# One order over a whole transformer block on one core, with TensorE's part in both arms of each block's branch

## The reference

```python
# 1: attention on Q, K, V reshaped to (B*H, S, D) = (64, 1024, 8); its output is projected, added and normed again
scores = jnp.einsum('bqd,bkd->bqk', Q, K) / jnp.sqrt(jnp.float32(D))
attn = jax.nn.softmax(scores, axis=-1)
ctx = jnp.einsum('bqk,bkd->bqd', attn, V)
# 2: a gated feed-forward with ternary weights, width 512
h = jax.nn.silu(_tlin(x, w1_w, w1_s)) * _tlin(x, w2_w, w2_s)
h = jax.nn.gelu(_tlin(h, h1_w, h1_s), approximate=False)
h = jax.nn.gelu(_tlin(h, h2_w, h2_s), approximate=False)
return _tlin(h, w3_w, w3_s)
# 3: gated linear attention, a scan over the time of each sequence
h = h * jnp.exp(gt)[..., None] + kt[..., None] * vt[..., None, :]
ot = jnp.einsum('bhk,bhkv->bhv', qt, h)
# 4: a mixture of 8 experts ("zones"); per sequence of 1024 rows the router takes the top 3
z = jax.nn.gelu(x @ Wa[e]) @ Wb[e]
zone_outputs = zone_outputs + z * w[:, e, None, None]
```

## Time and profile before

| | us |
|---|---|
| median of 3 runs | 1131.49 |
| lowest and highest of them | 1122.34, 1132.95 |
| the profiled execution | 1121.4 |
| its span, from the first to the last instruction | 1119.5 |
| PE busy | 1019.4 (91%) |
| ACT busy | 810.6 (72%) |
| DVE busy | 646.0 (58%) |
| POOL busy | 375.2 (34%) |

### The profile page before, as it was taken

The page is one execution under the profiler, slowest core; times in us unless marked ns, Lnnn a source line. Parts: engine busy times, 40 slices in busy tenths (PEclk is TensorE's granted clock), DMA queues, the critical chain, the costliest instruction groups (busy, mean ns, idle before and its releaser), DMA issues.

```text
span 1119.5 us, 16637 instructions
## 1 busy us (share of the span) xinstructions
PE 1019.4 (91%) x5970; PEld 509.1 (45%) x5970; DVE 646.0 (58%) x1173; ACT 810.6 (72%) x1097; POOL 375.2 (34%) x317
## 2 busy tenths in 40 slices
PE   2799999999999999999698988888788899999998
PEld 1232333333333333333276655565355536666667
DVE  3121454526344443313464999999999899995200
ACT  2699999999999999999557667565656675455441
POOL 1000010101000010100153787798679767655100
PEclk7799999999999999999899999999799999999999
DMA  5766453625455452710101101100000122011200
GB/s 126 121 113 118 92 117 63 125 60 110 77 104 96 86 106 52 121 36 15 34 1 38 38 1 39 38 1 29 28 20 1 57 57 85 1 48 29 57 29 20
DMA packets 98780, 66.90 MB, mean 60 GB/s; under 512 B 61636, under 2 KB 84964, under 8 KB 96612
## 3 DMA queue, kind: packets, MB, share of 16 engines
q1 hardware_dynamic: 98656, 65.33, 28.0%
q10 hardware_dynamic: 24, 0.25, 0.1%
HBM read 46.41 MB, written 18.87 MB: 58 GB/s over the span
## 4 chain that ended last, share of the span: by engine, by line
PE 63%; DVE 19%; POOL 5%; issue 5%; ACT 3%; SPq 1%; DMA 1%; ACTq 0%; DVEq 0%; POOLq 0%
PE PS L1481 26%; PE PS L1466 15%; DVE R L1293 8%; PE PS L1652 6%; PE PS L1515 4%; DVE R L1284 4%; POOL R L869 3%; PE PS L1641 3%; PE PS L1555 2%; PE PS L1410 2%; DVE RB L1246 1%; DVE R L1252 1%; PE PS L1579 1%; PE PS L1396 1%; DVE R L1256 1%
## 5 line engine op out<-in xcount | busy, mean ns | idle before, releaser
L922 ACT ACTIVATE R<-PS 128x1024 f32<-128x1024 f32 x512 | 474.4, 1085 | 58.4 <-PE PS L1466 57.6
L1481 PE MATMUL PS<-R 128*32 128x512 f32 x2048 | 314.1, 607 | 1.2 <-issue 1.2
L869 POOL TENSOR_TENSOR R<-R 128x512 f32<-128x512 f32 x128 | 216.1, 1705 | 50.0 <-DVE R L1293 27.1
L1293 DVE TENSOR_TENSOR_SCAN R<-R 128x512 f32<-128x512 f32 x128 | 208.6, 1630 | 0.0
L1466 PE MATMUL PS<-RA 34*128 34x512 f32 x1024 | 189.2, 447 | 20.1 <-DMA RA<-QD 19.5
L1515 PE MATMUL PS<-RB,WR 128*128 128x512 f32 x640 | 174.8, 417 | 18.4 <-DVE R L1252 12.1
L1466 PEld LDWEIGHTS PS<-RA 34*128 34x128 f32 x1024 | 77.1, 186 | 216.2 <-issue 193.5
L1515 PEld LDWEIGHTS PS<-RB,WR 128*128 128x128 f32 x640 | 122.9, 195 | 63.0 <-DVE R L1252 14.3
L1481 PEld LDWEIGHTS PS<-R 128*32 128x32 f32 x2048 | 68.0, 108 | 106.1 <-issue 94.1
L855 POOL TENSOR_TENSOR RB<-R,RB 128x512 fp32r<-128x512 f32 x48 | 75.6, 1576 | 76.6 <-ACT RB L932 68.1
L845 POOL PARTITION_ALL_REDUCE R<-R x8 | 3.0, 376 | 287.6 <-DVE R L1133 287.6
(11 more groups left out here) (129 smaller groups left out, 1005.1 us busy)
## 6 DMA issues: line engine op xcount, KB each, us to landing
RA<-QD SPq DMA_DIRECT2D x256, 64.0 KB
QD<-RA SPq DMA_DIRECT2D x128, 64.0 KB, 2.1
RA<-QD SPq DMA_DIRECT2D x64, 128.0 KB
OD<-R SPq DMA_DIRECT2D x128, 32.0 KB, 2.0
R<-OD SPq DMA_DIRECT2D x128, 32.0 KB
VD<-RC SPq DMA_DIRECT2D x16, 256.0 KB, 2.3
RC<-VD SPq DMA_DIRECT2D x16, 256.0 KB
WP<-in_Wa SPq DMA_DIRECT2D x12, 256.0 KB, 3.2
```

Source lines behind the costliest of these rows:

```text
L869: pool.tensor_tensor(st, st, Qc[b % 2], ALU.mult).then_inc(S["qh"], 1)
L922: act.activation(PR[u % 4], bank(2 * s, 1024), ACT.Exp, scale=SC).then_inc(S["exp"], 1)
L1293: dve.tensor_tensor_scan(st, Ac[k], st, CS[:, v:v + 1] if k else 0.0, ALU.mult, ALU.add).then_inc(S["scanned"], 1)
L1481: op = pe.matmul(bank(ob)[c:c + 32, :], VAF[b % 2][:, at:at + 32], PR[u % 4][:, 512 * h:512 * h + 512], start=(j == 0), stop=(j == 7), til ...
```

## The change

The attention loop becomes a stream of its own (`x`), and ORDER now interleaves it with the others from the first block on, so that steps 2 and 3 of a finished block run while later blocks are in attention. ORDER has 1,805 steps where it had 1,080; its rows would tell a reader nothing, so two lines of it stand below. With that come:

- PSUM: from pair 6 on (LATE) the units use two slots (banks 0 to 3), bank 4 is the only accumulator, and banks 5 and 6 serve all of steps 1 to 3 (`take`), bank 7 the gather. Two units' scores are issued together.
- The layout of keys and queries: the four score matmuls of two units use rows 0, 32, 64 and 96 of the array, 32 rows each, and the maxima are a separate accumulating matmul (L1451). PE's part of each block is emitted twice, in the two arms of a branch on the flag; the maxima and their matmuls stand in one arm.
- Buffers: three pairs' keys and queries instead of six, one output buffer OS instead of two, six states ST instead of ten, one Qc, Kc and Ac each instead of two, one stream for step 2 instead of two.
- The value rows of step 3 are spread by DMA from DRAM (`replica` on SP, 128 DMAs of 256 KB) and no longer by PE.
- The coarse parts in step 2 are cast by DVE; ACT no longer copies them or writes a gelu twice.
- `zone_down` is issued per hidden tile and not per 128 rows, with 13 hidden tiles in turn.

```diff
-NS = 10
+NS = 6
+NH = 13
+LATE = 6
...
 ORDER = (
-    "abcbbccbbccbbbacccbbbbbbbbacbbbbcacbcbcccbcapcbbcpbppbcpcppbpcpbcppbpppssssssbcssbcbscssssppsbssssbp"
+    "qqqxwqxxwxxxxwwxxxxxxxxxxxxxwlxxxxxxxxxxxxxwxxxqxxwxxxwxxxxfwxlxxfwxxxxwxxxxlxwxqxwxxxxwlxxxxxfxxxxx"
...
+    def take(self, who):
+
+        if self.acc < LATE:
+            return 6 + (self.acc + 1) % 2
+        banks = ((5, 6) if self.acc < 32 else
+                 {"b": (0, 1, 2), "d": (0, 1, 2), "o": (3, 4), "a": (4,), "c": (5, 6)}[who])
...
+    def stream_x(self):
+
         for pr in range(32):
...
             for w in range(8):
                 u = 16 * pr + 2 * w
                 self.add("scores", u)
-                self.add("scores", u + 1)
+                yield
                 if u >= 2:
                     self.add("weigh", u - 2)
                     self.add("weigh", u - 1)
...
             def load_pair(n):
-                b, i4, k = n // 4, n % 4, n % 6
+                b, i4, k = n // 4, n % 4, n % 3
...
-                if n >= 6:
-                    need.wait_ge("scores", 16 * (n - 5))
+                if n >= 3:
+                    need.wait_ge("scores", 16 * (n - 2))
...
+            def replica(b, v):
+                n = 16 * b + v
+                need.wait_ge("v_out", 16 * (b + 1))
+                if n >= NS:
+                    need.wait_ge("gather_ps", (n - NS) // 4 + 1)
+                if n >= 3:
+                    need.wait_ge("kv", n - 2)
+                sp.dma_start(ST[n % NS], bass.AP(VD.tensor, VD[b, 0, v, 0:1].offset,
+                                                 [[8192, 8], [0, 16], [1, 512]])).then_inc(S["rep_in%d" % (n % 3)], 16)
...
-            def scores(u):
-                pr, j, gg, b, g, s = unit(u)
-                need.wait_ge("scores", u + 1)
-                if u >= 4:
-                    need.wait_ge("pv", u - 3)
-                act.activation(PR[u % 4], bank(2 * s, 1024), ACT.Exp, scale=SC).then_inc(S["exp"], 1)
+            def scores(u0):
+                log_exp()
+                for u in (u0, u0 + 1):
+                    pr, j, gg, b, g, s = unit(u)
+                    need.wait_ge("scores", u + 1)
+                    if u >= 4:
+                        need.wait_ge("pv", u - 3)
+                    act.activation(PR[u % 4], bank(2 * s, 1024), ACT.Exp, scale=SC).then_inc(S["exp"], 1)
...
-                op = act.activation(HL[L][m][:, 1, :], bank(bk), ACT.Gelu, scale=sB[:, scale + m:scale + m + 1])
-                if scale < 12:
-                    op = act.activation(part(HL[L][m][:, 0, :]), bank(bk), ACT.Gelu,
-                                        scale=sB[:, scale + m:scale + m + 1])
-                op.then_inc(S["gelu"], 1)
+                act.activation(HL[L][m][:, 1, :], bank(bk), ACT.Gelu, scale=sB[:, scale + m:scale + m + 1]).then_inc(S["gelu"], 1)
...
-                dve.tensor_tensor(ST[n % NS], bank(3 + v % 2), Kc[b % 2], ALU.mult).then_inc(S["kv"], 1)
+                dve.tensor_tensor(ST[n % NS], ST[n % NS], Kc, ALU.mult).then_inc(S["kv"], 1)
...
+                slots = [(unit(u + gg)[5], gg) for gg in range(2)]
+                for s, gg in slots:
+                    for h in range(2):
+                        room(2 * s + h)
+                    for h in range(2):
+                        p = 32 * (2 * h + gg)
+                        op = pe.matmul(bank(2 * s + h), exact(KS[k][p:p + 32, 128 * j:128 * j + 128]),
+                                  exact(QS[k][p:p + 32, :]), start=True, stop=not guarded[0])
+                        emptied[2 * s + h] = ("exp", u + gg + 1)
+                    if not guarded[0]:
+                        op.then_inc(S["scores"], 1)
+                for s, gg in slots if guarded[0] else ():
+                    for h in range(2):
+                        p = 32 * (2 * h + gg)
+                        op = pe.matmul(bank(2 * s + h), view(GSEL[p:p + 8, n:n + 1], (0, 128)), exact(GQ[p:p + 8, :]),
+                                       start=False, stop=True)
+                    op.then_inc(S["scores"], 1)
...
-            def replica(b, v):
-                n, bk = 16 * b + v, 3 + v % 2
...
+            for b in range(NBLK):
+                need.wait_ge("flag", b + 1)
+                pe.reg_load(flag_reg, flags[0:1, b:b + 1])
+                met, held = dict(need.met), dict(emptied)
+                with pe.If_eq(flag_reg, 1):
+                    guarded[0] = True
+                    maxima(b)
+                    play(begins[b], ends[b])
+                need.met, guarded[0] = met, False
+                emptied.clear()
+                emptied.update(held)
+                with pe.Else():
+                    play(begins[b], ends[b])
+            play(ends[-1], len(order))
```

More of the change, by code:

```diff
@@ L82, in __init__ @@
         self.order, self.total = [], {}
[L83 to L87, removed]
+        self.done = {}
+        self.acc, self.turn, self.loaded = 0, {}, 2
+        self.weighed, self.closed = False, 0
         self.parts_of = {}
-        self.xt3, self.x3, self.xn = {}, {}, {}
-        self.attention()
+        self.xt3 = {}
+        self.start()
         self.rest()
@@ L98, in count @@
         return (name, self.total[name])
[L100 to L113, removed]
-        return e
@@ L177, in attention, with stats, apply, stats_shift @@
-    def attention(self):
-        self.stats("X", 0, 0, ("x_in0", 16))
+    def stats(self, k, where, b, *after):
+        n = self.count("bn_aggr_" + k)[1]
+        self.add("stats", k, where, b, n, self.done.get(k), after)
+        return n
+    def apply(self, k, to, where, b, n, *after):
+        e = self.done[k] = self.count("norm_" + k)
+        self.add("apply", k, to, where, b, n, e, after)
+        return e
+    def stats_shift(self, k, where, b, *after):
+        n = self.stats(k, where, b, *after)
+        self.add("shift", k, n)
+        return n
@@ new lines, in scale @@
+    def scale(self, k, to, where, b, n, *after):
+        e = self.done[k] = self.count("norm_" + k)
+        self.add("scale", k, to, where, b, n, e, after)
+        return e
+    def take(self, who):
[3 more added lines that the diff above has]
+                 {"b": (0, 1, 2), "d": (0, 1, 2), "o": (3, 4), "a": (4,), "c": (5, 6)}[who])
+        at = self.turn[banks] = self.turn.get(banks, -1) + 1
+        return banks[at % len(banks)]
@@ L229, in attention @@
                     self.add("finish", pr - 1)
-                if w == 2 and pr:
-                    self.add("fetch", pr - 1)
-                for step in plan.get(8 * q + w, []):
-                    step(6 + (pr + 1) % 2)
+                    self.acc = pr
+                yield
         self.add("weigh", 510)
@@ L278, in level @@
             self.parts_of[key] = [None] * 2
-            bk = self.take()
+            bk = self.take("b")
             done = self.count("hid_ps")
             hi = self.count("gelu")
+            if n0 == 6:
+                self.parts_of[key][0] = hi
             self.add("hid_mm", n0, b, m, [("hl", src, k) for k in range(4)],
-                     [list(self.parts_of[before, b, k]) for k in range(4)], bk, hi)
+                     [list(self.parts_of[earlier, b, k]) for k in range(4)], bk, hi)
@@ L1087, in _, with stats_ @@
             flag_reg = dve.alloc_register("flag_dve")
-            def stats_(where, b, k, n, before, after):
-                src = normed_tile(where, b)
+            def stats_(k, where, b, n, before, after):
+                src, j = normed_tile(where, b), LNS[k]
                 for e in after:
@@ L1661, in _, with play @@
                         gather=gather, mean_mm=mean_mm, out_c=out_c, turn_c=turn_c, route_1=route_1, route_2=route_2,
                         zone_up=zone_up, zone_down=zone_down)
-            for name, *at in order:
-                if name in does:
-                    does[name](*at)
+            def play(first, last):
+                for name, *at in order[first:last]:
+                    if name in does:
+                        does[name](*at)
+            begins = [i for i, step in enumerate(order) if step[0] == "guard"]
@@ new lines, in _ @@
+            ends = begins[1:] + [max(i for i, step in enumerate(order) if step[0] == "scores") + 1]
+            play(0, begins[0])
+            for b in range(NBLK):
+                need.wait_ge("flag", b + 1)
[10 more added lines that the diff above has]
+                    play(begins[b], ends[b])
```

1016 lines of the change are left out of this document (479 added, 537 removed).

## The result

| | before | changed |
|---|---|---|
| median, us | 1127.48 (4 runs, 1122.34 to 1132.95) | 1411.78 (4 runs, 1408.97 to 1416.36) |
| span of the profiled execution, us | 1119.5 | 1409.6 |
| ratio | | 1.2525 (95% interval 1.2443 to 1.2606) |

The changed kernel is slower by 284 us. The forecast was 1101 us, with a range up to 1165; no rival came near the result either. The page of the changed kernel, against the earlier trace rows: busy times; PE, DVE, ACT, the granted clock and the DMA share in 40 slices; the queue that carries nearly all bytes; the shares of the chain that ended last. PE's slices of the kernel before stand first.

A forecast was written before the change was run, and what follows sets the result against it. ACT was taken to bound attention, PE the tail. Start 34 + attention 748 x 1.066 (797) + branches 12 + tail 251 x 1.02 (256) = 1099, plus 1.9: 1101 us; range 1048 to 1165.

The forecast's parts named there:

- Replicas by DMA, shallower buffers: Value rows by DMA and fewer key and query buffers: no added time from DMA waits, issuing or buffer reach, each 0.
- Some 800 make 540 us of about 1100, so 0 as well: SP's queue: 8 DMAs issue in 5.42 us, some 800 take 540 us, so issuing costs 0.
- DVE's order leaves over 5 us a state, so 0: Step 3's value rows: asked for up to six states ahead, so waits for them cost 0, bound 74 us.
- The order's margin: Attention: 748 us by count times 1.066, the excess of the earlier trace over its count, gives 797 us.
- no gain: Rival, attention: ACT idles 9 to 10% in place of 6.6%, adding some 22 us: 1123 us; chance 0.15.
- scores come late: Rival, attention: two slots expose 0.80 us of ACT idle per pair of units: 1190 us, half 1146; chance 0.27.
- the first rival: Attention goes only 2% above its count, as the rest does now: 1057 us, 1050 to 1080; chance 0.18.
- The sign of late scores: In the waits, ACT's exponential would idle behind PE's scores for over 80 us.
- table loads: ACT: 136 loads for 48, each 1.28 us, 1.31 with gaps; the 88 more cost 115 us.
- PE's work: PE's load in attention: 660 us, below ACT's 748.
- waits of PE for DMA behind the first pairs: Sign that the forecast is wrong: PE waiting for DMA after the first pairs; no size given.
- The branches: PE's eight branches: each skips about 500 matmuls or more and costs 1.55 us, 12 us in all.

The follow-up runs named there:

- e1: The changed kernel with the repetition moved inward in the DRAM pattern of the key and query loads, rows and copies interleaved: 1233.13 us.
- e4: e1 with the values written twice to DRAM, so a value-row DMA has 16 outermost in place of 8: 1217.65 us.
- e5: e4 with keys and queries loaded for the first three pairs only: 1143.74 us.
- e11: e4 with every DMA kept, but later pairs' key and query loads bring 64 columns only: 1216.94 us.
- e12: e5 with the waits that stood ahead of each pair's loads put back on SP: 1150.95 us.
- e9: e5 with the value rows small as well, 8 of 128 rows of a state loaded: 1141.87 us.
- e7: e4 with PE's part of each block emitted once, without the branch and the maxima: 1214.47 us.
- e2: The changed kernel with small value rows, 8 of 128 rows of a state loaded, the others zero: 1364.44 us.
- e6: e4 with the value-row and weight DMAs issued by POOL in place of SP: 1217.73 us.
- e10: e4 with the weight loads alone issued by POOL in place of SP: 1214.47 us.
- e13: e4 with the four key DMAs of every pair kept, but the eight query DMAs for the first three pairs only: 1156.88 us.
- e3: The changed kernel with the repetition moved inward in the key loads alone, queries left as they were: 1235.65 us.

## Why the prediction was wrong

**The step that failed** is "Replicas by DMA, shallower buffers", with its three zeros. "Key and query buffers reach two pairs ahead, over 35 us: 0" counted only how early a buffer comes free. It did not cost the loads in their new form: by the rate above 14.6 us of transfer a pair, with all else of the same queue behind them. Their pattern is worth 179 us (e1), the largest term of all, and stood in the sum at nothing. Nor did the reach hold for every pair: SP comes to the loads of pair 12 at 371.89 us, and PE stands for them from 382 on. From the first load issued to the pair's first score it is under 35 us for 11 of the 29 later pairs, six of them the first of a block.

"Some 800 make 540 us of about 1100, so 0 as well" miscounted SP's work and took a half-busy queue for a free one. SP issues 974 DMAs in the changed kernel; 808 is the count before. The records of its DMA issues add up to 720 us there and 587 in e4 (424 before). And e5, e11 and e12 together leave 66 us for the DMAs of the loads whatever their size, at a share of SP of under half (587 of 1217 us). "DVE's order leaves over 5 us a state, so 0" for the value rows was wrong by 15 us for the spread over engines (e4), and left out waits of DVE of 117 us in e4, half of which go with the loads' DMAs. The 2.3 us of the earlier trace rows was that of a write; e4's page has 3.7 us for a value row's DMA.

**The order's margin** (1.066 times the count, 797 us, and 12 for the branches) was too small by 37 us: 846 in e9, where next to no bulk transfer is in the way. e9's 1142 lies between the rival "no gain" (1123) and the half case of "scores come late" (1146), and far from the first rival, as good as the rest does (1057). The sign of late scores, over 80 us of ACT's idle behind them, is just met: 82 us behind the first exponential, and 247 in the changed kernel, where late loads share in it. How much of the 37 us are late scores and how much the weight loads (DVE waits 54.7 us for them in e9) and short steps, no run separates. Nor did any run give back the third slot or the six pairs' buffers.

**Right were** ACT's work (742 us for 748), DVE's (512 for 540), the tail (263 for 256) and the table loads. There are 136 of 1283 ns, all 174.5 us. The Trainium skill's 2.66 us for a switch ("ScalarE: Activation LUTs", "What ACT_TABLE_LOAD costs") is not seen here either: in the changed kernel 107 of them have less than 0.2 us of idle both before and behind, with medians of 18 and 12 ns over all. PE's work was not right: 776 us in attention where 660 were counted, at a granted clock of 0.83; in e9 740 at 0.92. The clock may be a part of that miss; no run shows how much. Of the things named as wrong signs, "waits of PE for DMA behind the first pairs" came true: L1443 behind RA<-QD, 58.3 us.

**The branches** were put at 12 us and measure 3 or nothing (e7).

The account of the time, from the changed kernel down: 1411.8, less 178.7 (e1) for the loads' engines, 15.5 (e4) for the value rows', 73.9 (e5) for the rest of the loads, of which 66 go with their number, 7 with waits and 1 with bytes, and 1.9 (e9), gives 1141.9; the last 41 to the forecast are the order, with the tail's few us. The terms hold in this order of removal only: the value rows' bytes, 2 us here, are 47 when taken first (e2). The fastest versions tried that compute everything are e4, e6 and e10, 1214 to 1218 us and not told apart, 8% slower than before. What was not tried is a layout in DRAM that lets a pair be loaded in fewer DMAs; by e13 that would be the next place to look, and by e9, an estimate, it could come near the kernel before at best.

## What to carry to other kernels

Read every new access pattern of a DMA from its outermost dimension: a repetition belongs inside (one line for the keys' 128 KB loads was worth 179 us here), and a window with a low DMA share while something waits for a DMA is the sign. Cost a load by its issue, its transfer and what is queued ahead of and behind it, not by how far ahead its buffer is free. In an order that is strict on every queue, an issuing engine at half load can already delay (e4, 587 of 1217 us); count the issues a step adds, and make them fewer before moving them, since another engine's stream has steps of its own that others wait for.

## What the runs showed of the hardware that I had not expected

Eight issues took 5.96 us in e1 and 9.62 us in the changed kernel, of the same size and number (the chain has one of 3.08 us among others of 0.59). Over all 256 query DMAs the issues add up to 251.5 us in the changed kernel and 172.9 in e1, the median one 1.04 us and 0.66. It is not so behind every pair: pair 11's eight took 5.62 us. Nor is it the queries' own pattern, which e3 keeps: 154.8 us. What the runs show is that the issues got slower behind key DMAs with the repetition outermost; why, they do not show.

```profile
380.72 0.60 SPq L707
381.37 3.08 SPq L707
```

Cutting the later loads to a sixteenth of a key row and an eighth of a query row left the time where it was (e11, 0.7 us less), while dropping two thirds of the later DMAs took 61 us off (e13). And PE's mean granted clock in attention was lower where PE idled more: 0.83 in the changed kernel (776 us busy of 1112), 0.89 in e4 (762 of 922), 0.92 in e9 (740 of 846), with 1.00 in the tails of all three.
